# A four-layer graph network on one core: the next head's value columns in six pieces between the masks, and two stages made one

## The chip, the cores and the metric

One NeuronCore of a Trainium2 chip runs the whole program in one launch. The metric is the device time of a launch in microseconds (us), the median over runs; lower is better.

## What is computed

`x` is 2048 x 512, `adj` a 2048 x 2048 0/1 matrix. Four layers, each a residual around a normalized and rectified input `h = relu(layernorm(x))`:

```python
# layer 0: attention, 16 heads of 32; layer 2: the same form, 8 heads of 64, then a small MLP
seq = (h @ W).reshape(N, H, DH)
score = leaky_relu((seq @ a1)[:, :, None] + (seq @ a2)[:, None, :], 0.2)
attn = softmax(where(adj, score, -inf), axis=-1)
hidden = einsum('hij,jhd->ihd', attn, seq)
# layer 1: Y = h + sum over two steps of (R^s h) U1[s] + Xa[s] U2[s], Xa[s] = topp_softmax(...) Xa[s-1]
#          then layernorm(Y) * gamma + beta
# layer 3: sparse relation attention
```

## The kernel before

A program is a row of stages. Each stage opens its own buffers and semaphores and ends with a barrier of all engines (`Build.open`, L173 to L179). Each engine's program is written out in order by hand; semaphores tie them. TensorE multiplies, VectorE and ScalarE compute, SP issues loads, GpSimd some stores. The nodes are 16 tiles of 128 rows (`NT`), the features 4 blocks of 128 (`KD`).

**Attention stage** (`attention_stage`, called twice: 16 heads of 32 with `IB` = 8 and 2 chunks of output rows a head, then 8 heads of 64 with `IB` = 4 and 4 chunks). The leaky softmax is split: exp(leaky(s1 + s2)) is a product of a row factor and a column factor, with one pair of factors where the sum is positive and another where it is not. So a head needs, for each chunk and each of 16 neighbour tiles j, a 0/1 mask "edge, and sum positive". VectorE makes it: for 4 of 16 tiles in one instruction from the scores (L663), for 12 from a steep ramp of ScalarE (L578) by a minimum with the adjacency (L661). In the second attention 5 tiles also get the opposite mask (`other`, L672). TensorE multiplies each mask with the head's value columns (L721, L710, L715) and the adjacency with a third set (L728), and adds up in PSUM. Masks live in a ring of 8 (`RING`), opposite ones in a ring of 2. TensorE frees a slot when it has used it (`mask_used`).

The value columns `V` of a head are seq times the two column factors, in three bf16 parts each, made by VectorE in `columns` (L592 to L617): thresholds (L593, L594), then for each half of the tiles the products (L601 to L604), the first part and its rest (L606, L607), the second and third part and the negative (L608 to L611). `V` has two slots, but `columns` of a head runs as one block before that head's masks, and TensorE waits for it. `results` (L624 to L637) reduces a finished chunk at the tenth tile of the next one.

On SP, ScalarE, VectorE and TensorE the first two heads are straight code and the others a loop over pairs of heads (L544, L687); in the loop VectorE's addresses and wait values come from registers.

**Mixing stage** (`mix_stage`): per tile t, TensorE transposes A (L742), multiplies with U2 (L1816) and adds y by an identity matmul (L1818). VectorE normalizes (L1848 to L1863), and `RowNorm` makes the next layer's normalized, rectified and transposed input, 9 steps (`LAG`) behind (L125 to L159). SP loads y and x tiles four deep (L1776, L1779) and at the end the adjacency (L1786).

**Projection stage** (`project_stage`), second call: loads W and the attention vectors (L341, L347), VectorE folds these into score weights (L377, L380), TensorE computes seq (L448), the scores (L472) and their transposes (L480), with the first 8 tiles of seq before the scores. VectorE takes the maximum (L394), which goes through DRAM and back, and the exponentials close the stage (L434 to L437, L416).

Of the kernel before, what the change touches and what calls it, by code (L numbers as in the profile page):

```python
# [15 lines left out]
ALU = mybir.AluOpType  # L16
# [22 lines left out]
OTHERS = 2  # L39
TOP_P = 0.9  # L40
# [121 lines left out]
class Build:  # L162
# [322 lines left out]
    def attention_stage(self, H, DH, IB, relu_tiles, other_tiles, seq, hid, g, adj_in=None):  # L485
# [15 lines left out]
        with self.open() as st:  # L501
# [82 lines left out]
            def _(dve):  # L584
                base = [0, 0]

                def link(ins):
                    base[1] += 1
                    ins.then_inc(dve_done, 1)
                    dve.wait_ge(dve_done, base[0] + base[1])  # L590

                def columns(h, u):  # L592
                    dve.tensor_copy(thr_h[:, u, 0, :], g.thr[:, bass.ds(h, 1), :].rearrange("p o t -> p (o t)"))  # L593
                    ins = dve.tensor_copy(thr_h[:, u, 1, :], g.steep[:, bass.ds(h, 1), :].rearrange("p o t -> p (o t)"))  # L594
                    ins.then_inc(thr_ready, 1)
                    for half in range(2):
                        js = slice(half * HJ, (half + 1) * HJ)
                        sq = seq[:, js, bass.ds(h * DH, DH)]
                        cE = g.colE[:, bass.ds(h, 1), js].rearrange("p o t -> p (o t)")
                        cF = g.colF[:, bass.ds(h, 1), js].rearrange("p o t -> p (o t)")  # L600
                        dve.tensor_tensor(Vs[:, :, 0, 0:DH], sq, cE.unsqueeze(2).to_broadcast([P, HJ, DH]), ALU.mult)  # L601
                        dve.tensor_tensor(Vs[:, :, 1, 0:DH], sq, cF.unsqueeze(2).to_broadcast([P, HJ, DH]), ALU.mult)
                        dve.tensor_copy(Vs[:, :, 0, DH:C].rearrange("p t o -> p (t o)"), cE)
                        link(dve.tensor_copy(Vs[:, :, 1, DH:C].rearrange("p t o -> p (t o)"), cF))  # L604
                        p0, p1, p2 = (V[:, u, js, 0:2, part * C:(part + 1) * C] for part in range(3))
                        link(dve.tensor_copy(p0, Vs[:, :, :, :]))  # L606
                        link(dve.tensor_tensor(Vs[:, :, :, :], Vs[:, :, :, :], p0, ALU.subtract))  # L607
                        link(dve.tensor_copy(p1, Vs[:, :, :, :]))  # L608
                        link(dve.tensor_tensor(p2, Vs[:, :, :, :], p1, ALU.subtract))

                        ins = dve.tensor_scalar(V[:, u, js, 2, :], V[:, u, js, 1, :], -1.0, None, ALU.mult)  # L611
                        if half == 0:
                            link(ins)
                        else:
                            ins.then_inc(V_ready, 1)
                    dve.wait_ge(thr_ready, h + 1)
                    link(dve.memset(rec[:, 0:1], 1.0))  # L617

                def results(h, c, n):

                    b = c % 2
# [9 lines left out]
                    rE = g.rowE[:, bass.ds(h, 1), c * IB:(c + 1) * IB].rearrange("p o t -> p (o t)")  # L631
                    rF = g.rowF[:, bass.ds(h, 1), c * IB:(c + 1) * IB].rearrange("p o t -> p (o t)")
# [4 lines left out]
                    link(dve.tensor_tensor(hid[:, c * IB:(c + 1) * IB, bass.ds(h * DH, DH)], num[:, :, 0:DH],  # L637
                                           rec[:, :].unsqueeze(2).to_broadcast([P, IB, DH]), ALU.mult))

                per_pair = [None]  # L640

                def body(h0, first):

                    base[0] = 0 if first else h0 * (per_loop // 2) - per_chunk
                    base[1] = 0
# [41 lines left out]
                with dve.Fori(1, H // 2) as pair:  # L687
                    assert body(pair * 2, False) == per_loop
# [1557 lines left out]
```

## Time and profile before

| | |
|---|---|
| median of 3 runs | 4400.75 us (4398.19 to 4403.47) |
| the profiled execution | 4401.35 us, its span 4399.6 us |
| TensorE matmul busy | 3591.4 us, 82% of the span |
| VectorE busy | 3563.9 us, 81% |
| ScalarE busy | 2548.3 us, 58% |
| GpSimd busy | 1430.8 us, 33% |
| granted TensorE clock, mean | 0.895 |

The span goes from the first to the last instruction. Busy shares are means over stages with different limits, so each stage is looked at by itself. In the rows, PE is TensorE, PEld its weight loads, DVE VectorE, ACT ScalarE, POOL GpSimd and SP the SyncE queue; a "q" behind a name is the engine's sequencer. PEclk is the granted clock as a share of 2.4 GHz (0.5 is the 1.2 GHz level).

### The profile page before, as it was taken

How to read it: one execution, taken by the hardware profiler on the slowest of the kernel's cores; microseconds unless marked ns; L12 is line 12 of the kernel's file. 1: busy time of each engine (PE TensorE's matmuls, PEld its weight loads, DVE VectorE, ACT ScalarE, POOL GpSimd, SP SyncE). 2: the span in 40 equal slices, each digit the busy share in tenths (PEclk: the TensorE clock that was granted, in tenths of full speed). 3: DMA queues.
4: the chain of work that ended last, by engine and by line, in shares of the span. 5: the costliest groups of instructions: out<-in, count | busy, mean ns of one | idle time of the engine just before them, and what ended most of it. 6: DMA issues, size and time to landing. Idle time of an engine off the chain costs nothing. (4 is left out here: it accounts for less than half of the span.)

```text
span 4399.6 us, 57106 instructions
## 1 busy us (share of the span) xinstructions
PE 3591.4 (82%) x20136; PEld 2088.5 (47%) x20136; DVE 3563.9 (81%) x5868; ACT 2548.3 (58%) x3008; POOL 1430.8 (33%) x1417
## 2 busy tenths in 40 slices
PE   6788888879888747888888888788897977888887
PEld 3688888534344313333343343667674423333333
DVE  4799999769999994899999742888883169998996
ACT  3566666459889874788797712444452344444442
POOL 0444100017788783499879620000000100000000
PEclk9899999989999969899989999899898978888888
DMA  4611000211110101411101052000001211111110
GB/s 153 238 26 31 26 26 21 76 50 48 44 44 29 34 12 47 152 35 33 36 15 41 17 167 99 24 16 16 16 11 59 80 65 56 43 48 43 43 43 15
DMA packets 160244, 228.80 MB, mean 52 GB/s; under 512 B 85137, under 2 KB 96288, under 8 KB 154672
## 3 DMA queue, kind: packets, MB, share of 16 engines
q1 hardware_dynamic: 148592, 191.33, 13.4%
q0 software_dynamic: 11376, 33.76, 2.1%
q8 instruction: 177, 2.90, 0.3%
q14 instruction: 99, 0.81, 0.1%
HBM read 158.48 MB, written 66.47 MB: 51 GB/s over the span
## 5 line engine op out<-in xcount | busy, mean ns | idle before, releaser
L1684 DVE SCALAR_TENSOR_TENSOR junk<-expd,mid 128x2048 bf16<-128x2048 f32 x440 | 1036.1, 2355 | 13.8
L578 ACT ACTIVATE steepz<-s1b,thr_h 128x1024 bf16<-128x1024 f32 (+1 forms) x768 | 665.3, 926 | 538.7 <-DVE mask L661 462.3
L721 PE MATMUL acc<-V,mask 128*128 128x198 bf16 (+1 forms) x5504 | 754.4, 276 | 182.3 <-DVE mask L663 182.3
L1584 ACT ACTIVATE junk_s<-expd,nmid 128x2048 bf16<-128x2048 f32 x264 | 529.1, 2004 | 124.9 <-POOL nmid L1644 112.2
L721 PEld LDWEIGHTS acc<-V,mask 128*128 128x128 bf16 x5504 | 484.6, 100 | 241.7 <-DVE mask L663 140.4
L1587 ACT ACTIVATE junk_s<-expd,nmid 128x2048 bf16<-128x2048 f32 x264 | 528.3, 2001 | 0.0
L2003 PE MATMUL psS<-KT,qs 64*128 64x512 f32 x1024 | 382.0, 743 | 159.2 <-DVE m L2113 153.3
L728 PE MATMUL acc<-V,adjT 128*128 128x99 bf16 (+1 forms) x5504 | 454.6, 221 | 0.0
L661 DVE TENSOR_TENSOR mask<-steepz,adjT 128x1024 bf16<-128x1024 bf16 (+1 forms) x768 | 397.8, 553 | 28.9 <-PE acc L721 15.3
L728 PEld LDWEIGHTS acc<-V,adjT 128*128 128x128 bf16 x5504 | 370.5, 99 | 51.4 <-issue 3.1
L1456 PE MATMUL psX<-parts,block 128*128 128x512 bf16 x1536 | 368.1, 396 | 8.8 <-DMA block<-adj_dram 8.8
L1628 POOL TENSOR_SCALAR part<-signs,nmid 128x1 f32<-128x1 f32 x264 | 260.2, 986 | 218.0 <-ACT junk_s L1587 199.2
L1644 POOL TENSOR_SCALAR nmid<-reach,steps,nmid 128x1 f32<-128x1 f32 x216 | 301.8, 1397 | 22.7
L1629 POOL TENSOR_SCALAR sums<-part,above 128x1 f32<-128x1 f32 x264 | 300.4, 1138 | 26.6
L2003 PEld LDWEIGHTS psS<-KT,qs 64*128 64x128 f32 x1024 | 130.3, 219 | 360.5 <-DVE m L2113 247.0
L1969 POOL DMA_DIRECT2D out_dram<-xo x16 | 8.7, 541 | 839.7 <-DVE xo L2104 839.7
L2022 PE MATMUL psO<-B,attnT 128*128 128x512 f32 x512 | 268.7, 679 | 10.2 <-DVE xo L2104 10.2
L663 DVE SCALAR_TENSOR_TENSOR mask<-s1b,thr_h,adjT 128x1024 bf16<-128x1024 f32 (+1 forms) x256 | 259.5, 1014 | 18.1 <-PE acc L721 13.9
L2072 ACT ACTIVATE A<-A,nm 128x2048 f32<-128x2048 f32 x64 | 127.6, 1995 | 248.4 <-DVE nm L2119 248.4
L1441 PE MATMUL psX<-B,expd 128*128 128x512 f32 x512 | 236.7, 616 | 22.7 <-ACT expd L1546 17.0
L1441 PE MATMUL psX<-A,expd 128*128 128x512 f32 x512 | 235.3, 616 | 21.1 <-ACT B L1563 14.1
L1456 PEld LDWEIGHTS psX<-parts,block 128*128 128x128 bf16 x1536 | 156.2, 102 | 199.4 <-issue 38.4
(281 smaller groups left out, 5797.4 us busy)
## 6 DMA issues: line engine op xcount, KB each, us to landing
rows<-in_adj_dram SPq DMA_DIRECT2D x32, 1024.0 KB, 4.8
s1b<-sT_dram SPq DMA_DIRECT2D x32, 512.0 KB
block<-adj_dram SPq DMA_DIRECT2D x32, 512.0 KB, 4.4
adj_dram<-adjT POOLq DMA_DIRECT2D x4, 2048.0 KB, 20.1
rel_table<-zeros POOLq DMA_DIRECT2D x64, 128.0 KB, 19.5
y_dram<-yo SPq DMA_DIRECT2D x32, 256.0 KB, 2.0
step_dram<-xo SPq DMA_DIRECT2D x32, 256.0 KB, 2.0
A<-step_dram SPq DMA_DIRECT2D x8, 1024.0 KB, 13.7
```

The costliest lines, as they stand in the source:

```text
L578: act.activation(steepz[:, m % RELUS, :], s1b[:, q % 4, :], ACT.Relu, bias=thr_h[:, u, 1, j:j + 1], scale=STEEP).then_inc(relu_ready, 1)
L661: dve.tensor_tensor(out, steepz[:, m % RELUS, :], adj, ALU.min).then_inc(mask_ready, 1)
L721: mm = pe.matmul(acc[:, c % 2, i // TB, o:o + 2 * W], mask[:, j % RING, tile(i)], V[:, u, j, 0:2, :].rearrange("p s w -> p (s w)"), start= ...
L728: mm = pe.matmul(acc[:, c % 2, i // TB, o:o + W], self.adjT[:, j, tile(c * IB + i)], V[:, u, j, 2, :], start=False, stop=(last_in and i % ...
L1441: mm = pe.matmul(psX[:, bank["A", f], :], expd[:, slot[ends[f]], tile(j)], nat[:, j, :], start=(j == 0), stop=(j == NT - 1))
L1456: pe.matmul(psX[:, bank["S", t], :], block16[:, t % 2, j, :], parts[:, j, r, :], start=(j == 0 and r == 0), stop=False)
L1584: act.activation(junk_s[:, 0, :], expd[:, slot[i], :], ACT.Relu, bias=col(nmid, i), accum_out=col(above, i)).then_inc(sums_ready, 1)
L1587: act.activation(junk_s[:, 1, :], expd[:, slot[i], :], ACT.Sign, bias=col(nmid, i), accum_out=col(signs, i)).then_inc(sums_ready, 1)
L1629: link(pool.tensor_scalar(col(sums, i), col(part, i), -0.5, col(above, i), ALU.mult, ALU.add))
L1644: ins = pool.tensor_scalar(col(nmid, i), col(reach, i), steps[:, slot[i], f:f + 1], col(nmid, i), ALU.mult, ALU.add)
L1684: link(dve.scalar_tensor_tensor(junk[:, :], e, col(mid, i), e, ALU.is_gt, ALU.mult, accum_out=col(mass, i)))
L2003: mm = pe.matmul(psS[:, (n + b) % UNITS, c * 512:(c + 1) * 512], qs[r, t % 2, m, :], KT[r, m, o:o + 512], start=True, stop=True)
```

## The change

In `attention_stage`, VectorE's program is written out for every head, with constant addresses and wait values (SP, ScalarE and TensorE keep their loops). `columns` becomes six pieces that run after given masks of the head before: step number chunk x 16 + tile, from `COLUMNS`. TensorE waits for the first half of `V` at a head's start and for the second at tile 8. The last memset of `columns` is gone. `mix_stage` and the second `project_stage` become `mix_project_stage`: the projection of tile t - 13 (`BEHIND`) and the score groups are issued inside the mixing's steps, the second weights are loaded by SP after the fourth x tile, and VectorE folds the vectors in steps 6 to 13. The first `project_stage` stays.

```diff
+COLUMNS = {2: (12, 17, 20, 23, 28, 30), 4: (19, 27, 35, 43, 51, 59)}
...
+                def scaled(h, half):
+                    js = slice(half * HJ, (half + 1) * HJ)
+                    sq = seq[:, js, h * DH:(h + 1) * DH]
+                    cE, cF = g.colE[:, h, js], g.colF[:, h, js]
+                    dve.tensor_tensor(Vs[:, :, 0, 0:DH], sq, cE.unsqueeze(2).to_broadcast([P, HJ, DH]), ALU.mult)
+                    dve.tensor_tensor(Vs[:, :, 1, 0:DH], sq, cF.unsqueeze(2).to_broadcast([P, HJ, DH]), ALU.mult)
+                    dve.tensor_copy(Vs[:, :, 0, DH:C].rearrange("p t o -> p (t o)"), cE)
+                    link(dve.tensor_copy(Vs[:, :, 1, DH:C].rearrange("p t o -> p (t o)"), cF))
...
+                def first_part(h, half):
+                    link(dve.tensor_copy(part(h, half, 0), Vs[:, :, :, :]))
+                    link(dve.tensor_tensor(Vs[:, :, :, :], Vs[:, :, :, :], part(h, half, 0), ALU.subtract))
+
+                def other_parts(h, half):
+                    u, js = h % 2, slice(half * HJ, (half + 1) * HJ)
+                    link(dve.tensor_copy(part(h, half, 1), Vs[:, :, :, :]))
+                    link(dve.tensor_tensor(part(h, half, 2), Vs[:, :, :, :], part(h, half, 1), ALU.subtract))
+                    dve.tensor_scalar(V[:, u, js, 2, :], V[:, u, js, 1, :], -1.0, None, ALU.mult).then_inc(V_ready, 1)
+                    dve.wait_ge(V_ready, 2 * h + half + 1)
...
+                def columns(h, c, j):
+                    at = c * NT + j
+                    if at == COLUMNS[NC][0]:
+                        thresholds(h)
+                        scaled(h, 0)
+                    if at == COLUMNS[NC][1]:
+                        first_part(h, 0)
+                    if at == COLUMNS[NC][2]:
+                        other_parts(h, 0)
+                    if at == COLUMNS[NC][3]:
+                        scaled(h, 1)
+                    if at == COLUMNS[NC][4]:
+                        first_part(h, 1)
+                    if at == COLUMNS[NC][5]:
+                        other_parts(h, 1)
+
+                thresholds(0)
+                scaled(0, 0)
+                first_part(0, 0)
+                other_parts(0, 0)
...
+                for h in range(H):
+                    for c in range(NC):
+                        q = h * NC + c
+                        dve.wait_ge(s1b_in[q % 4], 16 * (q // 4 + 1))
+                        for j in range(NT):
+                            made(h, c, j)
+                            if j - 1 in other_at:
+                                opposite(h, c, j - 1)
+                            if q == 0 and j == HJ - 1:
+                                scaled(0, 1)
+                                first_part(0, 1)
+                                other_parts(0, 1)
+                            if j == RING + 1 and q >= 1:
+                                results((q - 1) // NC, (q - 1) % NC)
+                            if h + 1 < H:
+                                columns(h + 1, c, j)
+                results(H - 1, NC - 1)
...
-                        pe.wait_ge(V_ready, h0 + u + 1)
+                        pe.wait_ge(V_ready, (h0 + u) * 2 + 1)
...
+                                if c == 0 and j == HJ:
+                                    pe.wait_ge(V_ready, (h0 + u) * 2 + 2)
...
+            BEHIND = LAG + 4
+            scored = {18: 0, 20: 1, 22: 2, LAG + NT: 3}
...
+                    if t == 3:
+                        for k in range(KD):
+                            sp.dma_start(wp[:, k, :].rearrange("p (h d) -> p h d", h=H),
+                                         w_dram[:, tile(k), :].rearrange("h p d -> p h d")).then_inc(wp_in, 16)
+                        for i, v in enumerate((a1_dram, a2_dram)):
+                            sp.dma_start(avec[:, i, :, :], v.partition_broadcast(P)).then_inc(a_in, 16)
...
+                def sequence(t):
+                    if t == 0:
+                        pe.wait_ge(wp_in, 16 * KD)
+                    pe.wait_ge(norm.n_copied, t + 1)
+                    if t >= 2:
+                        pe.wait_ge(seq_copied, t - 1)
+                    for k in range(KD):
+                        mm = pe.matmul(psQ[:, t % 2, :], tr[:, k, tile(t)], wp[:, k, :],
+                                       start=(k == 0), stop=(k == KD - 1))
+                    mm.then_inc(seq_ready, 1)
...
-                for t in range(NT + LAG):
+                for t in range(NT + BEHIND):
...
+                    if LAG <= t < NT + LAG:
                         norm.turn(pe, t - LAG)
+                    if t in scored:
+                        scores(scored[t])
+                    if t >= BEHIND:
+                        sequence(t - BEHIND)
+                    if t == NT + BEHIND - 3:
+                        pe.wait_ge(sT_copied, 4)
...
+                        for u in range(NT):
+                            mm = pe.transpose(psS[:, u, :], sT[:, tile(u)], self.ident[0:2 * H, 0:2 * H])
...
+                    if t >= BEHIND:
+                        u = t - BEHIND
+                        act.wait_ge(seq_ready, u + 1)
+                        act.copy(nat[:, u, :], psQ[:, u % 2, :]).then_inc(seq_copied, 1)
...
+                    if 6 <= t < 6 + 2 * KD:
+                        fold(t - 6)
...
-            b.mix_stage(natA, trB, a["L1_gnn_U2_1"], step_dram, y_dram, xa, xb, adj_in)
...
-                b.project_stage(8, 64, a["L2_gnn_W"], a["L2_gnn_a1"], a["L2_gnn_a2"], natA, trB, g)
+                b.mix_project_stage(natA, trB, a["L1_gnn_U2_1"], step_dram, y_dram, xa, xb, adj_in,
+                                    8, 64, a["L2_gnn_W"], a["L2_gnn_a1"], a["L2_gnn_a2"], g)
```

## Rows read from the trace of the kernel before

**Rows 1.** Busy time by stretch: from and to, length, each engine, clock, DMA.
```profile
core 0: us, PE busy (x) PEld busy (x) DVE busy (x) ACT busy (x) POOL busy (x), PEclk, DMA share, GB/s
151.60:812.60 661.00, 564.71 (x8192) 558.38 (x8192) 627.16 (x1136) 408.11 (x384) 165.02 (x153) 0.91 0.16 53
151.60:191.30 39.70, 29.96 (x423) 29.68 (x424) 36.49 (x63) 25.61 (x24) 38.63 (x73) 0.82 0.97 383
191.38:231.17 39.79, 36.38 (x537) 36.03 (x535) 39.01 (x71) 25.50 (x24) 12.65 (x9) 0.96 0.39 136
2559.70:2663.00 103.30, 88.79 (x288) 45.77 (x288) 59.40 (x140) 31.95 (x69) 29.23 (x32) 0.91 0.74 259
2663.00:2750.20 87.20, 73.52 (x176) 29.23 (x176) 15.36 (x26) 14.03 (x25) 0.00 (x0) 0.91 0.09 20
2750.20:3311.80 561.60, 477.99 (x4096) 373.32 (x4096) 493.98 (x1128) 257.22 (x384) 0.00 (x0) 0.92 0.06 16
2818.10:2886.10 68.00, 59.76 (x514) 46.65 (x512) 61.81 (x142) 32.16 (x48) 0.00 (x0) 0.95 0.06 17
...
1840.00:1880.00 40.00, 36.84 (x126) 17.15 (x125) 38.52 (x57) 39.74 (x46) 34.73 (x34) 1.00 0.13 34
```

**Rows 2.** VectorE's timeline, first attention, head starts: start, us, what (heads 1, 2, 15).
```profile
191.46 0.16 DVE L594 COPY thr_h<-steep 128x16 f32<-128x16 f32 x1
...
231.25 0.17 DVE L594 COPY thr_h<-steep 128x16 f32 x1
...
763.75 0.17 DVE L594 COPY thr_h<-steep 128x16 f32 x1
```

**Rows 3.** VectorE's timeline, second attention: head starts 1, 2, 7, first mask, two reductions.
```profile
2818.19 0.17 DVE L594 COPY thr_h<-steep 128x16 f32<-128x16 f32 x1
...
2830.53 0.75 DVE L663 SCALAR_TENSOR_TENSOR mask<-s1b,thr_h,adjT 128x512 bf16<-128x512 f32 x1
...
2864.75 1.97 DVE L624 TENSOR_REDUCE sums<-acc 128x130 f32<-128x390 f32 x4
...
2879.19 1.97 DVE L624 TENSOR_REDUCE sums<-acc 128x130 f32<-128x390 f32 x4
...
2886.22 0.17 DVE L594 COPY thr_h<-steep 128x16 f32 x1
...
3234.60 0.17 DVE L594 COPY thr_h<-steep 128x16 f32 x1
```

**Rows 4.** TensorE's jump (ns min/median/max), then VectorE's issue waits, second attention and straight code.
```profile
L544 PEldq COMPARE_BRANCH  x10: 76/3594/5050, 316.2 to 3305.6; - x10
...
DVE thr_h L593 <- issue: 4.3, 2, 2.2
...
DVE KT L1232 <- issue: 0.4, 1, 0.4
```

**Rows 5.** TensorE's timeline: one mixing step, then the projection stage.
```profile
2617.91 0.60 PE L154 MATMUL psN<-ident,A 128*128 128x128 f32 x4
2618.35 0.60 PE L742 MATMUL psT<-ident,A 128*128 128x128 f32 x4
2618.78 3.60 PE L1816 MATMUL psO<-w,B 128*128 128x512 f32 x8
2622.22 1.02 PE L1818 MATMUL psO<-yt,ident 128*128 128x512 f32 x2
...
2672.28 30.72 PE L448 MATMUL psQ<-w,B 128*128 128x512 f32 x64 [10.53 <-DMA w<-in_L_gnn_W_dram]
2702.93 13.91 PE L472 MATMUL psR<-B,w 128*16 128x512 f32 x32
...
2728.37 17.43 PE L448 MATMUL psQ<-w,B 128*128 128x512 f32 x40
```

**Rows 6.** SP's issue of the second weights, and VectorE's first instruction of the second attention.
```profile
2664.59 4.35 SPq L341 DMA_DIRECT2D w<-in_L_gnn_W_dram  x4
...
2750.33 0.17 DVE L593 COPY thr_h<-thr 128x16 f32<-128x16 f32 x1 [1.24 <-PEq L179]
```

More of the change, by code:

```diff
@@ L584, in _ @@
             def _(dve):
[L585 to L615, printed above, removed]
-                    dve.wait_ge(thr_ready, h + 1)
-                    link(dve.memset(rec[:, 0:1], 1.0))
@@ new lines, in part @@
+                def part(h, half, r):
+                    return V[:, h % 2, half * HJ:(half + 1) * HJ, 0:2, r * C:(r + 1) * C]
+                def first_part(h, half):
[7 more added lines that the diff above has]
+                    dve.wait_ge(V_ready, 2 * h + half + 1)
@@ L622, in results @@
+                def results(h, c):
+                    n, b = h * NC + c, c % 2
                     dve.wait_ge(acc_ready, n + 1)
@@ new lines, in opposite @@
+                def opposite(h, c, j):
+                    q = h * NC + c
+                    m = q * OK + other_at[j]
+                    if m >= OTHERS:
+                        back = m - OTHERS
+                        dve.wait_ge(mask_used, (back // OK) * NT + other_tiles[back % OK] + 1)
+                    dve.wait_ge(mask_ready, q * NT + j + 1)
+                    dve.tensor_tensor(other[:, m % OTHERS, :], self.adjT[:, j, c * CI:(c + 1) * CI],
+                                      mask[:, j % RING, :], ALU.subtract).then_inc(other_ready, 1)
@@ L1802, in _, with scores @@
             def _(pe):
-                for t in range(NT + LAG):
+                def sequence(t):
[8 more added lines that the diff above has]
+                    mm.then_inc(seq_ready, 1)
+                def scores(c):
+                    if c == 0:
+                        pe.wait_ge(w12_ready, 1)
+                        pe.wait_ge(o_read, NT)
+                    pe.wait_ge(norm.n_copied, 4 * c + 4)
+                    if c >= 2:
+                        pe.wait_ge(sT_copied, c - 1)
+                    for k in range(KD):
+                        mm = pe.matmul(psO[0:2 * H, c % 2, :], w12[:, k, :, :].rearrange("p i h -> p (i h)"),
+                                       tr[:, k, c * D:(c + 1) * D], start=(k == 0), stop=(k == KD - 1))
+                    mm.then_inc(sT_ready, 1)
+                for t in range(NT + BEHIND):
                     if t < NT:
```

157 lines of the change are left out of this document (104 added, 53 removed).

## The prediction

> **What bounds the kernel now.** I read the trace by stages first: the busy time of each engine in the four stretches that the diff touches [rows 1]. To be seen there: in the first attention VectorE is busy 627 of 661 us, in the second 494 of 562, and the mixing and the projection after it are TensorE's (89 of 103 and 74 of 87). The rest of the program is not touched.
>
> Next the head starts on VectorE, the copy of the thresholds at L594 [rows 2, 3]. In the first attention a head of the straight part takes 231.25 - 191.46 = 39.79 us, of which VectorE is busy 39.01 [rows 1]: it is the bound, and TensorE (36.4 busy) waits. The 13 heads after it, in the loop, take (763.75 - 231.25) / 13 = 40.96 us. In the second attention the straight head takes 68.0 us, with VectorE busy 61.8 and TensorE 59.8: neither is full. The reason is the columns block: from 2818.19 to 2830.53 VectorE makes no mask, TensorE runs dry and starts again at the low clock level (granted clock 0.95 over the head). After that TensorE is the bound: two chunks' reductions are 14.44 us apart [rows 3], so 4 x 14.44 = 57.8 us of matmul work a head. In the loop a head takes (3234.60 - 2886.22) / 5 = 69.68 us.
>
> **First attention: the columns in six pieces.** Nothing is removed from VectorE; the same copies, products and differences run between masks. Where VectorE is the bound, it matters little where they stand. So this part gives nothing but the wait in head 0, where VectorE is busy 36.5 of 39.7 us [rows 1]: TensorE now starts after half the columns and is not yet behind. I take 3 us, between 0 and 3.2. The memset and its wait at L617 go: under 0.1 us a head.
>
> **First attention: program per head.** The 14 looped heads cost 40.96 - 39.79 = 1.17 us more than the straight one with the same work [rows 2]: register work before the reductions and columns. Straight code takes that away: 16.4 us. Together 20 us, between 16 and 22. TensorE's 36.4 us stay inside the new 39.7 us, so it does not take over.
>
> **Second attention.** New head: VectorE 61.8 less the memset, 61.6 us; TensorE 57.8. VectorE becomes the bound, with 3.8 us to spare. Eight times 61.6 is 493. Two things come on top. In the last head VectorE has no columns to make (12.3 us less, 49.3), so TensorE's 57.8 decide: 8.5 us. At the start TensorE runs at the low level for a few matmuls: 2 us. That is 504. What covers a piece: the longest is some 2.6 us (a quarter of the block's 12.3 would be 3.1), and eight masks in the ring are 8 x 14.44 / 16 = 7.2 us of TensorE.
>
> TensorE's own program stays a loop, and this is where a cost comes into view. Its jump back takes 3.6 us in the middle and 5.05 at most [rows 4]. Today it lies under the wait for the columns. Some 1 us of it passes beside matmuls already issued (an estimate; no row shows it), so 2.6 to 4 us are bare. There are two taken jumps in the second attention, at heads 4 and 6. A head's first chunk has no piece in it, so VectorE runs ahead, the ring of eight fills, and the delay is passed on: 5 to 8 us, I take 6. New stage 510, against 561.6: 51.6 us gained, between 42 (each jump 5 us, and 4 us of ring waits) and 58 (jumps hidden). In the first attention the six jumps fall into 3 to 5 us of spare time a head; 0 to 4 us there, I take 0.
>
> The Trainium skill (Advanced Engine Details and Errata, Control Flow Timing) gives a compare-and-branch about 108 ns. By it the jump would cost nothing and the stage would be 504; the row of TensorE's jump says 3.6 us, so the trace decides against it. VectorE's jump is short, but two heads of the second attention begin with 2.2 us of "issue" [rows 4]; straight code saves these, inside the 69.68 above.
>
> **Mixing and projection in one stage.** TensorE's order is the same up to step 12, which ends at 2628.7: the matmuls of step 11 end at 2623.1, its norm transposes take 0.43, and step 12 takes 0.43 + 3.44 + 0.86 + 0.43 = 5.17 [rows 5]. After it stand 3 transposes of 0.43, 4 mixings of 3.44 + 0.86, 12 norm transposes of 0.43, 4 score groups of together 13.9, 16 projections of 3.44 and the 16 small transposes of 1.1: 1.3 + 17.2 + 5.2 + 13.9 + 55.0 + 1.1 = 93.7. Before the last score group TensorE waits for ScalarE, which copies a projection and then the last norm tile: 1.2. That ends at 2723.6. Before, it ended at 2728.37 + 17.43 = 2745.8, and the attention began 4.5 us later, at 2750.33 [rows 6]: exponentials, barrier. With the same tail it now begins at 2728.1: 22 us gained. What goes is idle TensorE: 10.53 us for the weights [rows 5], one barrier, the norm's drain.
>
> What could be late next. The queue: the second weights and vectors are now issued by SP before the fifth y tile. Issue took 4.35 us and landing 7.7 (2664.59 to 2672.28) [rows 5, 6] on a quiet queue; here DMA is busy 0.74 of the whole stage [rows 1]. The y tile is needed some 13 us after that place in the queue. I count 0, up to 4. VectorE: the 16 folding instructions move into steps 6 to 13, 1.45 us a step, where VectorE is busy 59.4 of 103 us [rows 1]; 0 to 2 us. ScalarE now waits in each step for the projection, but its next transposed tile was due a step earlier; 0. The maximum, its trip through DRAM and the exponents' arguments are done while TensorE does the last two projections. So 16 to 23 us. The adjacency load is issued where it was and has over 80 us.
>
> **Sum.** 20 + 51.6 + 22 = 94 us. The profiled execution took 4401.35 (span 4399.6, 1.75 around it), so 4307.4; the median of the runs is 0.6 lower, which makes 4307.
>
> **Rivals.**
> - The clock falls in short waits. Each head of the second attention now has some 2 us of TensorE waiting in place of 8. If each wait brings the low level, each of 7 heads loses what a restart costs now (68.0 - 57.8 - 8.5 of waiting = 1.7, say 2): 4321. Against it: from 1840 to 1880 TensorE is busy 36.8 of 40 us, with gaps, and the granted clock is 1.0 [rows 1]. For it: nothing shows a head with just such gaps.
> - The merged stage waits: y tiles behind the weights, or the folding. Price 6 us: 4313.
> - VectorE's long straight code stalls as the loop did, 2.2 us once a head [rows 4]: 24 x 2.2 = 53 us, 4360. Against it: in the straight code from 840 to 2560 all "issue" waits of VectorE are 0.4 us. The Trainium skill (Advanced Engine Details and Errata, ISA Cache) speaks for it: outside TensorE's, the cache holds two lines of 256 instructions, so long code always loads new ones, and a loop of fewer than 512 does not. The trace agrees as to the loops, since the first attention's shorter one has no such wait.
> - The columns' move does nothing: VectorE is short of time in any case, and heads of the second attention stay at 68.0. Only the loop's 1.68 us for six heads is gained there: 20 + 10 + 22, 4349. Against it: VectorE is idle 6.2 us in such a head.
> - Slower. TensorE, now waiting a little all the time in both attentions, stays at the low level. All of it would be 16 x 70 + 8 x 115.6 = 2045 us in place of 1150. It decides from about a fifth of the matmul work at the low level: TensorE's 35 (36.4 x 0.96) and 57.8 us would grow to 42 and 69.2, which eats the 94 us. Against it: heads with 8.5 us waits still have 0.95.
>
> **How the numbers follow.** The forecast, 4307 with its own range of 4297 to 4318: 0.60. Short waits and clock 0.12, the merged stage waiting 0.10, straight code 0.05, no use of the move 0.04, slower 0.04; 0.05 for what I don't see, most of it still faster. The low end is all the upper bounds together (22 + 58 + 23 = 103: 4298), the high end takes in 4321 with the jumps at their dearest: 4297 to 4330 holds 0.82. Faster by over 0.2% (8.8 us, about what a measurement can tell) 0.93, within 0.03, slower 0.04.
>
> **What would show it.** Head starts 39.7 us apart in the first attention and 61.6 in the second; after two heads of the second a TensorE wait of "issue" or a jump of 3 to 5 us, followed by VectorE waiting for TensorE; no "issue" wait on VectorE; the attention starting 22 us sooner after the mixing begins, with TensorE without gaps from 2570 on. The prediction is wrong if VectorE waits for TensorE in the middle of a head of the second attention, if the granted clock there is under 0.97, or if the y tiles come late.

## The result: 4335.6 us, a gain of 66 us where 94 were forecast

| | before | after |
|---|---|---|
| median | 4402.1 us | 4335.6 us (4331.9 to 4338.0, four runs) |
| ratio | | 0.985 (0.983 to 0.987) |
| profiled execution, its span | 4401.35, 4399.6 | 4338.02, 4336.3 |
| mean granted TensorE clock | 0.895 | 0.91 |

The median of before was 4398.5 to 4402.1 us in the sessions of the study; each ratio is taken with the runs of before on the same chip. The kernel is faster, but by some 29 us less than forecast. The time lies 5.6 us above the end of the forecast's wider range (4330) and 17.6 above the end of its own (4318).

In words, the lengths of the stages in the two profiled executions. An attention is counted from VectorE's first instruction in it to the end of its last, the mixing and projection from the first mixing matmul to the second attention's first copy. The first attention went from 660.8 to 657.6 us (20 us of gain forecast, 3.3 came), the mixing and projection from 181.6 to 164.0 (22 forecast, 17.7 came), the second attention from 561.4 to 515.0 (51.6 forecast, 46.4 came). The untouched stages moved by +0.1 us in the middle and by +4.2 us behind the second attention. This last stretch takes 1084.5 to 1092.1 us in the profiled executions of this document, all with the same work there; the changed kernel's profiled one is the longest of them, and also the slowest of its four runs. I read nothing into it.

Busy time by stretch after the change, to be laid beside [rows 1]. The lines are the first attention, the mixing and projection from the same point as there, the second attention, then single heads of the second, each from one copy of the thresholds to the next: one without a jump of TensorE and two with one.

```profile
core 0: us, PE busy (x) PEld busy (x) DVE busy (x) ACT busy (x) POOL busy (x), PEclk, DMA share, GB/s
151.30:808.90 657.60, 572.17 (x8192) 557.22 (x8192) 630.84 (x1120) 414.84 (x384) 153.61 (x153) 0.95 0.16 53
...
2559.70:2729.10 169.40, 157.11 (x464) 71.85 (x464) 80.88 (x170) 45.63 (x94) 29.22 (x32) 0.97 0.49 164
2729.10:3244.20 515.10, 475.46 (x4096) 365.79 (x4096) 487.27 (x1120) 255.04 (x384) 0.00 (x0) 0.98 0.06 18
```
```profile
2752.06:2813.80 61.74, 58.67 (x513) 45.21 (x512) 60.60 (x142) 31.85 (x49) 0.00 (x0) 1.00 0.06 18
2937.50:3003.60 66.10, 60.20 (x511) 45.89 (x509) 60.79 (x141) 31.78 (x49) 0.00 (x0) 0.97 0.06 18
...
3065.80:3131.44 65.64, 59.77 (x508) 45.50 (x506) 60.98 (x141) 32.21 (x49) 0.00 (x0) 0.97 0.07 19
```

A head of the second attention takes 61.7 us with VectorE busy 60.6: VectorE is the bound and TensorE runs at the upper level throughout, as forecast. The two stretches with a jump take 4.4 and 3.9 us more. From a head's first mask to the next head's, heads 4 and 6 take 66.6 and 66.5 us, the others behind head 0 61.8. In the first attention VectorE's busy time is where it was (627 before, 631 now), so 27 us of idle time are left there, where the forecast length of 641 us would leave 10.

**Where the first attention lost it.** From first mask to first mask, heads without a jump of TensorE now take 39.9 us (heads 9, 11 and 13: 39.90, 39.90, 39.89). The heads with a jump differ: heads 4 and 6 take 40.4 and 40.1, heads 8, 10, 12 and 14 take 42.4, 42.1, 42.3 and 42.6. These four cost 9.8 us together. Before, the looped heads took 40.85 to 41.2. The jump's own row, TensorE's sequencer, minimum, median and longest in ns [rows 4 had 76/3594/5050]:

```profile
L545 PEldq COMPARE_BRANCH  x10: 76/4728/5422, 319.1 to 3238.0; - x10
```

The jump that begins at 480.73 takes 5.2 us. TensorE's timeline around it, start and length in us, and in brackets the idle time:

```profile
480.34 0.52 PE L739 MATMUL acc<-V,adjT 128*128 128x99 bf16 x8
480.69 0.85 PE L732 MATMUL acc<-V,mask 128*128 128x198 bf16 x8
481.38 0.52 PE L739 MATMUL acc<-V,adjT 128*128 128x99 bf16 x8
486.29 1.50 PE L732 MATMUL acc<-V,mask 128*128 128x198 bf16 x8 [4.39 <-DVE mask L646]
487.58 0.87 PE L739 MATMUL acc<-V,adjT 128*128 128x99 bf16 x8
488.25 1.52 PE L732 MATMUL acc<-V,mask 128*128 128x198 bf16 x8
```

The trace names a mask as what ended the wait, but that mask had been done long before; the wait is the jump. Behind it eight matmuls take 1.50 us in place of 0.85: the clock has gone to its lower level, 1.2 GHz (granted clock 0.53 from 486.29 to 492.20, and 0.91 over the head). Then the ring of masks is full, and VectorE waits:

```profile
484.35 1.89 DVE L646 TENSOR_TENSOR mask<-steepz,adjT 128x1024 bf16<-128x1024 bf16 x3
487.83 1.28 DVE L648 SCALAR_TENSOR_TENSOR mask<-s1b,thr_h,adjT 128x1024 bf16<-128x1024 f32 x1 [1.59 <-PE acc L732]
489.81 0.69 DVE L646 TENSOR_TENSOR mask<-steepz,adjT 128x1024 bf16<-128x1024 bf16 x1 [0.70 <-PE acc L732]
```

1.59 + 0.70 = 2.3 us of the head's excess of 2.5. And why 5.2 us, where [rows 4] had a median of 3.6? The traffic of the DMA queues in the same microseconds, three windows: 480.70 to 481.40, 481.40 to 483.60, 483.60 to 484.70.

```profile
q1 hardware_dynamic: 3, 0.01, 4.6%
issues: line engine op xcount, KB each, median us to landing
s1b<-sT_dram SPq DMA_DIRECT2D x1, 512.0 KB, 3.7
```
```profile
q1 hardware_dynamic: 140, 0.51, 65.9%
```
```profile
q8 instruction: 1, 0.02, 5.5%
```

The columns are packets, MB and the share of the 16 DMA engines. SP issues a head's score rows (`s1b`, 512 KB), 140 packets pass, and only behind them comes the one packet of 16 KB on the instruction queue, which I take for TensorE's code. The view does not name the engine, but such a packet comes in every one of these jumps. SP's issue and TensorE's jump now fall together, at the end of a head. Before, the same two were 2.4 us apart (477.7 and 480.06): most of the rows' packets had passed when the code's was asked for, and it started 0.9 to 1.3 us after each jump.

**Where the merged stage lost it.** TensorE's waits between 2584 and 2640 after the change, and further down the end of its program:

```profile
2589.28 1.12 PE L1896 MATMUL psO<-yt,ident 128*128 128x512 f32 x2 [0.57 <-DMA yt<-y_dram]
2621.01 0.63 PE L155 MATMUL psN<-ident,A 128*128 128x128 f32 x4 [1.32 <-ACT B L160]
2627.18 0.63 PE L155 MATMUL psN<-ident,A 128*128 128x128 f32 x4 [0.81 <-ACT B L160]
2633.23 0.63 PE L155 MATMUL psN<-ident,A 128*128 128x128 f32 x4 [0.70 <-ACT B L160]
```
```profile
2706.01 3.61 PE L1877 MATMUL psO<-B,w 128*16 128x512 f32 x8 [1.16 <-ACT B L160]
...
2717.71 7.13 PE L1865 MATMUL psQ<-wp,B 128*128 128x512 f32 x16
```

The wait at 2706 was in the forecast (1.2 us). The four before it, 3.4 us of idle time, were not. From start to start of the matmuls around them they cost 4.0 us, since the modelled ends overlap the next start a little. The first is a y tile behind the weights: SP's issue of the four weight loads took 10.75 us here, against 4.35 in [rows 6], and the next y tile was issued at 2584.16. The other three are VectorE, which falls behind while it folds the vectors:

```profile
2621.00 0.69 DVE L126 BATCH_NORM_STATS2 stats<-xo 128x6 f32<-128x512 f32 x1
2621.73 1.93 DVE L1975 TENSOR_TENSOR prod<-wp,avec 128x512 f32<-128x512 f32 x1
2623.70 0.69 DVE L1977 TENSOR_REDUCE w<-prod 128x8 f32<-128x512 f32 x1
2624.42 0.70 DVE L1950 BATCH_NORM_STATS2 stats<-psO 128x6 f32<-128x512 f32 x1
```

It has no idle time, and the product takes 1.93 us where its undisturbed neighbours take 0.68. In the same moment GpSimd runs a product of its own, 1.28 us from 2621.83. The Trainium skill (SBUF — State Buffer, section SBUF: two separate sides) says that a VectorE instruction with two operands in SBUF, as this product is, and a GpSimd instruction that reads SBUF take turns at a shared port, for a whole instruction each. Its own length and GpSimd's, 0.68 + 1.28 = 1.96 us, agree with the 1.93 measured.

### The profile page after: what moved, and what is told of

Same layout as the page of the kernel before. It is cut to its first block and busy times, and to the rows that moved or that the text cites. A ratio compares the mean times of both kernels' runs of the same rounds, so it can differ in the third digit from the quotient of the medians.

```text
span 4336.3 us, 55622 instructions
## 1 busy us (share of the span) xinstructions
PE 3594.6 (83%) x20081; PEld 2079.6 (48%) x20136; DVE 3571.6 (82%) x5848; ACT 2553.4 (59%) x3008; POOL 1425.2 (33%) x1417
## 5 line engine op out<-in xcount | busy, mean ns | idle before, releaser
L1467 PE MATMUL psX<-parts,block 128*128 128x512 bf16 x1481 | 354.6, 393 | 13.5 <-DMA block<-adj_dram 10.7
L1639 POOL TENSOR_SCALAR part<-signs,nmid 128x1 f32<-128x1 f32 x264 | 278.6, 1055 | 214.1 <-ACT junk_s L1598 194.4
L1640 POOL TENSOR_SCALAR sums<-part,above 128x1 f32<-128x1 f32 x264 | 277.7, 1052 | 26.6
```

The costliest lines, as they stand in the source:

```text
L1467: pe.matmul(psX[:, bank["S", t], :], block16[:, t % 2, j, :], parts[:, j, r, :], start=(j == 0 and r == 0), stop=False)
```

## The experiments

Theory one was, from here on: the shortfall is TensorE's jumps (of which the long ones wait for their code behind score rows) and, in the merged stage, the folding and the early load. Stage lengths in us, from the profiled executions:

| kernel | median, ratio (95%) | first attention | mixing, projection | second attention |
|---|---|---|---|---|
| before | 4400 | 660.8 | 181.6 | 561.4 |
| after | 4335.6, 0.985 (0.983 to 0.987) | 657.6 | 164.0 | 515.0 |
| pe_straight | 4316.8, 0.981 (0.980 to 0.983) | 647.5 | 164.1 | 505.8 |
| scores_late | 4320.1, 0.982 (0.980 to 0.984) | 648.2 | 163.7 | 510.7 |
| one_block | 4362.4, one run | 646.8 | 164.0 | 550.2 |
| fold_late | 4334.8, 0.985 (0.983 to 0.987) | 657.8 | 165.9 | 515.3 |
| merge_alone | 4385.2, 0.997 (0.996 to 0.998) | 660.0 | 164.5 | 563.3 |
| attention_alone | 4344.3, 0.988 (0.986 to 0.990) | 653.0 | 180.4 | 513.1 |
| no_marks | 4331.5, one run | 657.8 | 164.1 | 511.5 |
| fold_mid | 4332.7, one run | 658.2 | 160.7 | 513.3 |
| straight_fold | 4314.2, 0.981 (0.979 to 0.982) | 647.2 | 160.5 | 506.1 |
| block_first | 4314.1, 0.980 (0.979 to 0.981) | 646.6 | 161.5 | 505.9 |

**TensorE without jumps.**

```diff
-                pairs(pe, body)
+                for h0 in range(0, H, 2):
+                    body(h0, h0 == 0)
```

> The changed kernel with TensorE's program of both attentions written out for every head, as VectorE's is; nothing else. Theory one, the jump: in the changed kernel every second head from head 8 of the first attention takes 42.3 us in place of 39.9, and heads 4 and 6 of the second 66.5 in place of 61.8, each behind a jump of TensorE of 4.7 to 5.4 us. Without jumps 4 x 2.4 + 2 x 4.7 = 19 us go: first attention heads all at 40 to 40.6 us, second all at 61.8, 4317 us. Theory two, long code: what costs time is loading new code, and straight code for TensorE has to be loaded all the time; then a wait of some 4 us comes about once in two heads whatever the loop, and the time stays at 4336 or rises to 4350.

Measured: 4316.8. Both attentions came out as expected, 10.1 and 9.2 us shorter: the jumps, and with them the loop's register work on TensorE, cost 19 us of the changed kernel's time. A head of the second attention that had followed a jump is now like the others:

```profile
2719.38:3225.10 505.72, 471.93 (x4096) 364.07 (x4096) 486.72 (x1120) 254.88 (x384) 0.00 (x0) 0.99 0.06 18
...
2989.50:3051.40 61.90, 58.76 (x515) 45.29 (x513) 60.75 (x141) 31.82 (x49) 0.00 (x0) 1.00 0.07 18
```

**The score rows issued eight masks later, the jumps kept.**

```diff
-                                sp.wait_ge(mask_ready, h0 * SH + (q - 3) * NT)
+                                sp.wait_ge(mask_ready, h0 * SH + (q - 3) * NT + HJ)
```

> The changed kernel with SP's load of the next score rows (s1b) held back by half a chunk, eight masks later; TensorE keeps its loop. Theory one, a shared queue: the code that TensorE's jump loads stands behind the 512 KB of score rows that SP issues 0.4 us before the jump (before the change it was issued 2.4 us before and was done). Then the jumps at heads 8 to 14 of the first attention shrink from 5.1 us to 3.4 to 3.7 and cost 0 to 0.5 us each: 8 to 9 us less there; in the second attention the two jumps shrink from 4.7 by 1 to 1.5 us: 2 to 3 us less, together about 4325 us. Theory two: the jump is long because TensorE is starved or because of the code it goes to, whatever SP does; jumps stay at 5 us and the time at 4336 us.

Measured: 4320.1; all six jumps of the first attention took 3.57 to 3.74 us. Of the heads behind them 8, 10 and 14 cost nothing and 12 cost 0.7 us; 4 and 6 (40.7 and 40.6) lie close to their neighbours, which took 40.2 to 40.5. The stage is 0.7 us longer than without any jump, so nearly all that the jumps cost in the first attention comes from their being long. TensorE's timeline at the same jump as above:

```profile
478.21 0.85 PE L732 MATMUL acc<-V,mask 128*128 128x198 bf16 x8
478.90 0.52 PE L739 MATMUL acc<-V,adjT 128*128 128x99 bf16 x8
482.23 0.85 PE L732 MATMUL acc<-V,mask 128*128 128x198 bf16 x8 [2.81 <-DVE mask L648]
482.92 0.54 PE L739 MATMUL acc<-V,adjT 128*128 128x99 bf16 x8
```

And the queues from 478.25 to 480.60 in this kernel, where the code's packet is alone with some tiny ones of GpSimd:

```profile
q0 software_dynamic: 32, 0.00, 4.4%
q8 instruction: 1, 0.02, 3.4%
```

A wait of 2.8 us, and the matmuls behind it still take 0.85 us: here the clock did not fall. A jump 1.6 us longer costs the head 2.5 us more. In the second attention the first jump took 3.32 us and cost its head 1.7; the other stayed long (4.95 us) with no score rows near it. In that case two code packets of 16 KB were under way at once; which engine's the other was I did not establish. The same is seen at two more long jumps, that of 5.05 us in the kernel before, which is the maximum of [rows 4], and one of 4.66 us in the kernel in one block. The two packets take 1.4 to 2.3 us there, where one alone takes 0.9 to 1.4. The stage took 510.7 us, between that of the changed kernel and that without jumps.

**The columns in one block, everything else as changed.**

```diff
-COLUMNS = {2: (12, 17, 20, 23, 28, 30), 4: (19, 27, 35, 43, 51, 59)}
+COLUMNS = {2: (31,) * 6, 4: (63,) * 6}
```

> The changed kernel with all six pieces of the next head's columns after the last mask of a head, so that they are one block again; straight code for VectorE and the merged stage stay. Theory one, the pieces carry the second attention: its heads go from 61.8 back to 68.0 us, the jumps hide under the block again, so the stage takes about 515 + 6 x 6.2 - 9 = 543 to 550 us and not 515; the first attention, where VectorE is full anyway, does not mind: heads of 39.9 us, and the jumps cost nothing, 8 to 10 us less than now. In all about 4336 + 31 - 9 = 4358 us. Theory two, straight code carries it: heads of the second attention near 62 us with one block as well, 4330 us.

Measured: 4362.4. A head of the second attention takes 68.1 us, so the pieces are worth 6.3 us in each of its heads. In the first the block with straight code takes 646.8 us, 10.8 us less than the pieces. Two things go together there: the block hides the jumps, and they are short, 3.3 to 3.7 us, since SP issues the score rows 3.1 to 4.2 us ahead of them. TensorE's restart after the block in the second attention, to be compared with the 0.83 us of these four matmuls at full clock:

```profile
2867.41 1.48 PE L732 MATMUL acc<-V,mask 128*128 128x390 bf16 x4 [8.26 <-DVE mask L648]
```

**The folding in steps 13 to 16 of the merged stage, two a step.**

```diff
-                    if 6 <= t < 6 + 2 * KD:
-                        fold(t - 6)
-                    if t == 6 + 2 * KD:
+                    if 13 <= t < 13 + KD:
+                        fold(2 * (t - 13))
+                        fold(2 * (t - 13) + 1)
+                    if t == 13 + KD:
```

> The changed kernel with the folding of the attention vectors moved from steps 6 to 13 (one pair of instructions a step) to steps 13 to 16 (two pairs a step), where a step of TensorE is 8.6 us long. Theory one, VectorE late: it falls behind in steps 6 to 13, so that TensorE waits 1.3, 0.8 and 0.7 us for the norm copies at steps 11 to 13. These waits go, 2.8 us less in the merged stage, its length from the first mixing matmul to the attention's first instruction 164.0 to about 161.2 us; in all 4333 us. Theory two, loads late: the x tiles stand behind the second weights in SP's queue (GpSimd waited 6.3 us for one), and VectorE is late by that; then the waits stay, 164.0 us.

Measured: the stage took 165.9 us, 1.9 more than before this edit and not less, so the expectation missed. The waits in steps 11 to 13 are gone, but a new one stands where the scores begin:

```profile
2668.09 5.30 PE L1877 MATMUL psO<-B,w 128*16 128x512 f32 x8 [3.44 <-DVE shift L1991]
```

TensorE is at step 18 before VectorE has finished step 17, and the first score group also runs at the lower clock (5.30 us against 3.61). The folding was the cause of the old waits, and I had put it too late. Not all of the 1.9 us is its doing: the first mixing group, ahead of any folding, took 5.58 us here and 4.60 in the changed kernel, since more of it ran at the lower clock level. Against that the wait for the y tile is gone, though the weights are loaded where they were.

**Either half of the change alone.** The first is the attention of before with the merged stage, the second the new attention with the two stages of before.

```diff
-            b.mix_stage(natA, trB, ...)
...
-                b.project_stage(8, 64, a["L2_gnn_W"], ..., natA, trB, g)
+                b.mix_project_stage(natA, trB, ..., 8, 64, a["L2_gnn_W"], ..., g)
```

> The attention program of the kernel before, with the merged mixing and projection stage. Theory one (the two halves of the change are independent of each other): the stretch between the last layer norm of the first layer and the second attention falls from 181.6 to about 164 us as in the changed kernel, both attentions stay at 660.8 and 561.4 us, so the time is 4402 - 17.7 = 4384 us. Rival (the merged stage hands the second attention a TensorE that waits or a program whose code is further away, and part of what the stage gains is lost at head 0): the second attention comes out longer than 561.4 by 3 us or more and the time is 4388 or above.

Measured: 4385.2; the stages are those of theory one, and the second attention is 1.9 us longer, below the rival's 3. The time alone does not decide: its runs of before had a median of 4398.5, so the gain is 13.3 us, where theory one gives 17.7 and the rival at most 14. The interval of the gain is 8 to 18 us and holds both.

> The attention program of the changed kernel, with the mixing and the projection in two stages as before. Theory one: the first attention takes 657.6 us and the second 515.0 us, as in the changed kernel, the stretch between the mixing's start and the second attention stays at 181.6 us, so the time is 4402 - 3.3 - 46.4 = 4352 us. Rival (the long jumps of TensorE, 4.8 to 5.4 us, depend on where the code lies in memory and not on SP's score rows): the jumps of this program come out at 3.3 to 3.7 us in some heads and the first attention at 648 to 655 us.

Measured: 4344.3, 8 us below what theory one gave (4 us below if one starts from its own runs of before, 4398.5). The first attention took 653.0 us and its jumps 4.85, 3.32, 3.29, 5.71, 3.56 and 4.40 us. So the rival's numbers came. Its mechanism did not: at each jump of this run the trace shows score rows in the same microseconds, and what differs is which comes first. I took the starts of the packets from the traces of the five kernels with pieces and jumps, 30 jumps of the first attention. In 21 the rows go first: their first packet starts 0.62 to 0.82 us after the jump (once 1.01), the code's packet only after 2.4 to 3.4 us, when 109 to 144 of the 144 have passed, and the jump takes 4.75 to 5.7 us. In 9 the code's packet starts 0.91 to 1.01 us after the jump, together with the first of the rows (0.88 to 1.08), and the jump takes 3.3 to 3.6 us, once 4.4 (its packet took 2.1 us). In all 30 the jump ends 1.25 to 1.50 us after the code's packet, so the packet sets its length. The order follows SP's issue: it begins 0.14 to 0.33 us before the jump in the 21 and 0.06 to 0.09 us before it in the 9. Why an edit moves it by such a tenth is open. In the changed kernel itself, head 6 (jump at 399.9) is of this kind; its queues from 400.60 to 401.30:

```profile
q1 hardware_dynamic: 25, 0.10, 53.4%
q8 instruction: 1, 0.02, 8.2%
```

It is a race that a tenth of a microsecond decides, so any edit that shifts it can move the first attention by several us. The two gains, each against its own runs of before, are 13.3 and 54.2 us, together 67.5; the whole change gave 66.5. The halves add up, within intervals of 5 and 7 us either way.

**GpSimd's marks in the relation table left out, but for one chunk.**

```diff
-        for c in range(C):
+        for c in range(1):
```

> The changed kernel with one of GpSimd's chunks of marks in the relation table instead of all (the rest of the marks is left out). Theory one (GpSimd's work beside VectorE costs the first attention's heads 1 to 7 half a microsecond each): those heads fall from 40.46 to 39.9-40.0 us, the first attention from 657.6 to 653.5-654.5 us, heads 8 to 15 unchanged. Rival (the excess of heads 1 to 7 is the descriptors' DMA traffic or TensorE's order, not GpSimd beside VectorE): they stay above 40.3 us and the first attention at 657 us or more.

Measured: heads 1, 2, 3, 5 and 7 of the first attention take 39.89 us (40.46, 40.64, 40.48, 40.46 and 40.5 with the marks), so the marks cost VectorE some 0.6 us a head. The edit takes away GpSimd's work and its small DMAs together; that VectorE's casts are themselves shorter without it, in the lines below, speaks for the engines being in each other's way. The stage nevertheless takes 657.8 us. Heads 4 and 6 now have long jumps as well (4.91 and 5.14 us) and take 42.1 and 42.3: what VectorE gained was lost to the race. The first cast of a head's columns, from 212 to 454 us, count, sum in us and mean in ns, with the marks and then without:

```profile
L607 DVE CAST V<-Vs 128x528 bf16<-128x528 f32 x12 | 6.6, 546 | 0.0
```
```profile
L607 DVE CAST V<-Vs 128x528 bf16<-128x528 f32 x12 | 5.1, 429 | 0.0
```

**The folding in steps 10 to 15, the weights loaded in step 7.**

```diff
-                    if t == 3:
+                    if t == 7:
                         for k in range(KD):
                             sp.dma_start(wp[:, k, :]...
...
-                    if 6 <= t < 6 + 2 * KD:
-                        fold(t - 6)
-                    if t == 6 + 2 * KD:
+                    if 10 <= t < 14:
+                        fold(t - 10)
+                    if 14 <= t < 16:
+                        fold(2 * t - 24)
+                        fold(2 * t - 23)
+                    if t == 16:
```

> The changed kernel with the folding of the score vectors in steps 10 to 15 of the merged stage (one each in 10 to 13, two each in 14 and 15) in place of steps 6 to 13, and the load of the projection weights in step 7 in place of step 3. Theory one (the folding beside GpSimd's products makes VectorE late in steps 6 to 13, and the load's issue makes SP late with the mixing's rows; both go with this placement and the first score group no longer waits as it did with the folding in 13 to 16): the stage takes 160.0 to 161.5 us instead of 164.0, the rest unchanged. Rival (VectorE has no room at all in the stage, so that the folding's 8 to 15 us show wherever it lies): 163.5 to 166 us, with the wait at another step.

Measured: 160.7 us, 3.3 less, and SP's issue of the weights back at 4.14 us:

```profile
2593.85 4.14 SPq L1824 DMA_DIRECT2D wp<-in_L_gnn_W_dram  x4
```

TensorE's only waits in the stage behind its first matmul are 0.58 us before the scores and the known 1.16. Load and folding were moved together here, so their shares are told apart only by the waits that went: 0.57 us of the y tile and 2.8 us of the folding. The first of these was no constant of the old place either. With the load in step 3 it was absent from the runs scores_late, fold_late and no_marks, and 1.0 us in merge_alone.

**Both repairs, and the pieces in the second attention only.** The first kernel is TensorE's straight program with the folding and load just shown. The second is the same with

```diff
-COLUMNS = {2: (12, 17, 20, 23, 28, 30), 4: (19, 27, 35, 43, 51, 59)}
+COLUMNS = {2: (31,) * 6, 4: (19, 27, 35, 43, 51, 59)}
```

> The changed kernel with TensorE's program of the attentions written out for every pair of heads (no jumps) and with the folding in steps 10 to 15 and the load of the projection weights in step 7 of the merged stage. Theory one (the two repairs lie in different stages and add up): first attention 647.5 us, stage ahead of the second attention 160.7 us, second attention 505.8 us, so 4316.8 - 3.3 = 4313.5 us. Rival (the longer program or the later load costs elsewhere what the stage gains): 4316.8 us or above.

> As the kernel beside it in this call, but with the next head's value columns of the first attention in one block behind the head's last mask; the pieces stay in the second attention. Theory one (with two passes per head VectorE sets the first attention's pace at 39.9 us a head with pieces or without, and only the jumps made the pieces a loss there): the first attention takes 646.5 to 647.8 us and the time is the same, 4313 us within 3. Rival (the pieces shorten the first attention's head, or spare it low-clock columns, as they do in the second): the first attention comes out longer than 650 us and the time above 4317 us.

Measured: 4314.2 and 4314.1 us; first attentions 647.2 and 646.6. These are the fastest kernels of the study, 21 us under the changed one and 86 under the one before. In the first attention the pieces are worth nothing once TensorE does not jump. The clock moves without moving the time: granted 0.96 with the pieces, 0.92 with the block, since TensorE has time to spare there.

```profile
151.37:797.93 646.56, 568.88 (x8192) 562.32 (x8192) 628.37 (x1120) 407.79 (x384) 167.79 (x153) 0.92 0.16 54
```

## Why the prediction was too optimistic

The direction and the order of the three parts were right; their sum of 94 us was 29 too high.

**First attention, 20 forecast, 3.3 measured.** The step that failed is "In the first attention the six jumps fall into 3 to 5 us of spare time a head; 0 to 4 us there, I take 0." Four of the six cost 9.8 us by the heads, all of them 10.1 by the run without jumps. For jumps of the length that the forecast read, 3.6 us, it would have held: with the score rows later all six cost 0.7 us. Two things were missing in it. TensorE's spare time in a head is no store that a jump can draw on: what counts is how many masks of the ring of eight are already waiting when TensorE stops (four take VectorE 3.0 us, 481.35 to 484.35 above, so the whole ring holds 6.0 us). A wait of 2.8 us passes under that, one of 4.4 us with a restart at the lower clock does not. And the jump's length was read from a trace in which SP's load came 2.4 us ahead of it. The change brought the two together, a moved step that I had not followed through SP's queue, and four jumps became 4.9 to 5.4 us long. The other 6.6 us are sizes. A looped head costs 40.86, a straight one 39.90, so 0.96 us and not 1.17: I had compared one head, 0.1 us short of 39.90, with an average that lay 0.1 us high by the heads beside GpSimd's marks (14 x 0.21 = 2.9 us). Head 0 begins its masks 3.2 us sooner but is itself 1.7 longer, so 1.5 of the 3 came. The rest, about 2.2, is what heads 2 to 7 lose more than before to GpSimd's marks; the run without marks shows that cost, its split between before and after is a difference of heads.

**Second attention, 51.6 forecast, 46.4 measured.** Columns under the masks, VectorE as the bound, the head at 61.6 us: right. Without jumps the stage takes 505.8 us, for a forecast of 504. The term that was mis-sized is the jumps, 6 us for two; they cost 9.2 (515.0 - 505.8), 4.6 each in place of 3. The jumps are 4.7 us long, for the same reason as in the first attention: the score rows (256 KB here) start 0.8 us after the jump, and the code's packet comes at 2.4. Of their length 1.9 us pass beside matmuls already issued, where the forecast estimated 1, so the bare wait, 2.9 us, lies inside the forecast's 2.6 to 4. What the 6 us did not contain is the restart at the lower clock. The sign that the forecast named is there; TensorE and then VectorE in the changed kernel's second attention, head 3 to 4:

```profile
2987.07 0.50 PE L739 MATMUL acc<-V,adjT 128*128 128x195 bf16 x4
2990.45 1.48 PE L732 MATMUL acc<-V,mask 128*128 128x390 bf16 x4 [2.88 <-issue]
2991.72 0.86 PE L739 MATMUL acc<-V,adjT 128*128 128x195 bf16 x4
```
```profile
2991.97 0.75 DVE L648 SCALAR_TENSOR_TENSOR mask<-s1b,thr_h,adjT 128x512 bf16<-128x512 f32 x1 [2.97 <-PE acc L732]
2993.93 0.42 DVE L658 TENSOR_TENSOR other<-adjT,mask 128x512 bf16<-128x512 bf16 x1 [1.21 <-PE acc L726]
```

The Trainium skill's compare-and-branch of about 108 ns (Advanced Engine Details and Errata, Control Flow Timing) does not hold for TensorE's jump, which the row gives as 4.7 us. For the short loops of SP and ScalarE in the same kernel nothing speaks against it: their jumps took 40 to 55 ns.

**Mixing and projection, 22 forecast, 17.7 measured.** The order and the count of matmuls were right. Two costs that the prediction names and sets at "0, up to 4" and "0 to 2 us" were 0.6 and 2.8 by the idle rows, and 4.0 together from start to start. The clock hid some more: the first mixing group ran 0.9 us faster than in the kernel before (4.60 against 5.50), so some 1 us of the shortfall stays without a row. For the second cost I had averaged VectorE's busy time over the old stage (59.4 of 103 us) and taken the products at their undisturbed length; GpSimd's product beside them makes them up to three times as long. With both moved the stage takes 160.7 us, against 181.6 - 22 = 159.6 by the forecast.

**Sum.** 16.7 + 5.2 + 4.3 = 26.2 us of the shortfall lie in these three terms. The other 2.4 are differences between executions: the last stretch, 4.2 us longer in the profiled one, less the 2.4 us by which the median lies below it, and rounding.

**The rivals.** "The clock falls in short waits" did not come about: heads of the second attention without a jump have a granted clock of 1.00, and the stage 0.98. "The merged stage waits" (price 6 us) is right in kind and about two thirds in size (4.0); the late y tile was one of the forecast's own signs of being wrong. "Straight code stalls" is refuted for both engines: 647.5 and 505.8 us with TensorE in straight code as well. The Trainium skill (Advanced Engine Details and Errata, ISA Cache) gives the cache of the other engines two lines of 256 instructions; by that such code would be loaded all the time. The run without jumps agrees as to the loading. Its first attention has 64 packets of 16 KB of code (packets, MB, share):

```profile
q8 instruction: 64, 1.05, 0.7%
```

But no wait of VectorE or TensorE goes with it. What waited in these runs was the taken jump. That straight code finds its next part already loaded is the reading that fits, and no row shows it directly.

"The columns' move does nothing" fell with the run in one block: 6.3 us a head in the second attention. For the first attention that rival was true.

## What to carry to other kernels

A jump's cost in a trace is the cost at the place where it stands now. When the change takes away what covers it, look at three things: how far the next engine's ring reaches, what else is issued to the DMA queues in that microsecond, and at which clock level the engine comes back. If the program has room, write the loop out: here that is worth 19 us.

Small helper work put "beside" a stage has to fit into the steps in which it lies, not into the stage's average, and its durations should be taken from rows in which the same neighbours are busy.

Where one engine is the bound, as VectorE is in the first attention, moving its work about gains nothing and can lay other costs bare.

## What the runs showed that was not expected

- A jump of TensorE takes 3.3 to 4.05 us in the first attention when its code's 16 KB packet starts 0.9 to 1.3 us after the jump (once 4.4, where the packet itself took 2.1 us). It takes 4.75 to 5.7 us when the packets of 512 KB of score rows came first, and a tenth of a microsecond in SP's issue decides which. In all 30 jumps looked at it ends 1.25 to 1.50 us after the code's packet.
- A wait of 2.81 us left the clock at the upper level in the first attention; after one of 4.39 us eight matmuls took 1.50 us for 0.85. In the second attention a wait of 2.88 us was enough for the lower level (1.48 us for 0.83). Two equally long waits of one stage even ended differently, so these rows give no rule. From the first attention of the run without jumps:

```profile
473.89 0.85 PE L732 MATMUL acc<-V,mask 128*128 128x198 bf16 x8 [2.94 <-DVE mask L646]
673.42 1.50 PE L732 MATMUL acc<-V,mask 128*128 128x198 bf16 x8 [2.94 <-DVE mask L646]
```

- A DMA issue on SP is not of fixed length: the same four weight loads took 10.75 us to issue in step 3 (10.3 to 10.9 in six other runs), 4.14 in step 7 and 4.35 in a quiet stage [rows 6].
- A faster kernel on one side can lose the gain to a race on the other: without GpSimd's marks (one run) five heads ran 0.6 us faster each, two others 1.7 to 2.2 slower, and the stage stayed at 657.8 us.
